# Two expert stages of a decoder kernel: inner rows made already turned, with the expanding weights fetched per row tile

## What is computed

```python
def moe_ff(x, gate_w, w1, w2, w3):            # layer L1_ffn: 8 experts, the best 2, inner width 512
    scores = xf @ gate_w
    topk_scores, topk_idx = jax.lax.top_k(scores, TOPK)
    topk_probs = jax.nn.softmax(topk_scores, axis=-1)
    ...
    h = jax.nn.silu(einsum('td,edh->eth', xf, w1)) * einsum('td,edh->eth', xf, w2)
    out_e = jnp.einsum('eth,ehd->etd', h, w3)
    out = jnp.einsum('etd,te->td', out_e, weight)
...
# layer L2_ffn: 8 experts, the best 1, inner width 1024
expert_idx = jnp.argmax(gate_probs, axis=-1)
for e in range(n_experts):
    ye = jax.nn.relu(x @ w1[e] + b1[e]) @ w2[e] + b2[e]
    out = out + jnp.where(sel, ye * expert_w[:, None], 0.0)
```

## Time and profile before

| | |
|---|---|
| median of three executions | 3069.21 us (3069.16 to 3077.27) |
| profiled execution, span from first to last instruction | 3070.0 us |
| TensorE busy | 2724.3 us, 89% of the span |
| VectorE, ScalarE, GpSimd busy | 1635.4, 1435.2, 1409.9 us |
| mean granted TensorE clock | 0.942 of full speed |
| moved by DMA | 106.09 MB, 35 GB/s on average |
| tile loop of stage a | 1369 to 1602 us, 39 tiles |
| tile loop of stage b | 2365 to 2553 us, 23 tiles |

### The profile page before, as it was taken

One profiled execution on the slowest core, in us unless ns is written; L12 is line 12 of the kernel. 1 busy time (PEld: TensorE's weight loads), 2 busy tenths in 40 slices (PEclk: granted clock), 3 DMA queues, 4 the chain that ended last, 5 costly groups with the idle time before them and its releaser, 6 DMA issues.

```text
span 3070.0 us, 70943 instructions
## 1 busy us (share of the span) xinstructions
PE 2724.3 (89%) x25041; PEld 2119.4 (69%) x25041; DVE 1635.4 (53%) x3572; ACT 1435.2 (47%) x4582; POOL 1409.9 (46%) x1645
## 2 busy tenths in 40 slices
PE   7888988569899979969986889999996996999999
PEld 6777776446666656746655767787774665768888
DVE  7999999654356645551126753333333224556643
ACT  4666665444366657733327852222321335773310
POOL 3777777723466755543335652332322223663320
PEclk9999998779999999969997989999995998999999
DMA  3000000100000000141111020000016111010100
GB/s 99 3 2 2 2 2 2 55 30 1 23 15 17 14 20 1 55 146 43 45 64 47 0 94 11 7 10 10 7 54 220 33 32 52 1 48 29 53 10 20
DMA packets 75141, 106.09 MB, mean 35 GB/s; under 512 B 11024, under 2 KB 54672, under 8 KB 74656
## 3 DMA queue, kind: packets, MB, share of 16 engines
q1 hardware_dynamic: 68960, 86.68, 8.5%
q0 software_dynamic: 5952, 16.26, 1.7%
HBM read 88.50 MB, written 14.42 MB: 34 GB/s over the span
## 4 chain that ended last, share of the span: by engine, by line
PE 55%; POOL 4%; DVE 4%; ACT 3%; issue 3%; SPq 1%; DMA 1%; DVEq 0%; ACTq 0%; POOLq 0%
PE up_ps L2490 5%; PE e_out_ps L2508 5%; PE t_ps L664 4%; PE s_ps L650 3%; PE bank_a L1554 3%; PE bank_b L1554 3%; POOL probs L569 2%; PE up_ps L2484 2%; PE bank_a L612 2%; ACT probs L798 2%; PE bank_d L701 2%; PE frame_ps L1633 2%; PE bank_d L620 2%; PE bank_b L1570 2%; PE bank_a L1570 2%
## 5 line engine op out<-in xcount | busy, mean ns | idle before, releaser
L569 POOL TENSOR_TENSOR probs<-probs,inv 128x512 f32<-128x512 f32 x320 | 328.0, 1039 | 274.1 <-DVE inv L919 273.9
L3454 POOL TENSOR_TENSOR hc<-h,bc 128x1024 f32<-128x1024 f32 x128 | 302.0, 2360 | 112.5 <-DVE h L3735 86.4
L798 ACT ACTIVATE probs<-s_ps,negmax 128x128 f32<-128x128 f32 (+1 forms) x768 | 297.7, 415 | 6.4 <-DVE negmax L879 5.0
L3735 DVE TENSOR_TENSOR_SCAN h<-da,dbu_ps 128x1024 f32<-128x1024 f32 x128 | 292.5, 2286 | 11.1 <-DVE dbu_ps L3747 4.4
L664 PE MATMUL t_ps<-ident,probs 128*128 128x128 f32 x1280 | 208.2, 286 | 57.8 <-POOL probs L569 49.2
L664 PEld LDWEIGHTS t_ps<-ident,probs 128*128 128x128 f32 x1280 | 139.2, 141 | 124.7 <-POOL probs L569 59.4
L3682 ACT ACTIVATE da<-dta_ps 128x1016 f32<-128x1016 f32 x128 | 130.3, 1018 | 150.2 <-PE dta_ps L3544 149.9
L3544 PE MATMUL dta_ps<-dt,a_spread 32*128 32x128 f32 x2048 | 155.2, 291 | 43.1 <-ACT da L3682 23.0
L2414 POOL DMA_INDIRECT expert_rows_out<-y,row_to x62 | 61.1, 986 | 268.7 <-DVE y L2773 138.3
L879 DVE TENSOR_REDUCE negmax<-s_ps 128x4 f32<-128x1024 f32 (+1 forms) x128 | 156.6, 1223 | 44.7 <-PE s_ps L650 42.7
L3544 PEld LDWEIGHTS dta_ps<-dt,a_spread 32*128 32x128 f32 x2048 | 130.4, 194 | 67.2 <-ACT da L3682 30.0
(11 more groups left out here) (509 smaller groups left out, 6752.4 us busy)
## 6 DMA issues: line engine op xcount, KB each, us to landing
cT<-in_ctx_turned SPq DMA_DIRECT2D x32, 256.0 KB, 2.6
w_down<-in_L_ffn_w SPq DMA_DIRECT2D x8, 1024.0 KB, 12.3
w_up<-in_L_ffn_w SPq DMA_DIRECT2D x8, 1024.0 KB, 13.5
c_in<-in_ctx SPq DMA_DIRECT2D x16, 256.0 KB, 2.8
w_gate<-in_L_ffn_w SPq DMA_DIRECT2D x8, 512.0 KB, 6.8
w_up<-in_L_ffn_w SPq DMA_DIRECT2D x8, 512.0 KB, 9.0
w_down<-in_L_ffn_w SPq DMA_DIRECT2D x8, 512.0 KB, 9.0
w_gate<-expert_rows_out SPq DMA_DIRECT2D x8, 512.0 KB, 6.6
```

What stands on the lines that cost most here:

```text
L569: pool.tensor_tensor(probs[:, u % 2, i], probs[:, u % 2, i], inv[:, u % 2, HB * i:HB * (i + 1)].unsqueeze(2).broadcast_to([P, HB, W]), ALU ...
L798: last = act.activation(probs[:, u % 2, i, k, :], src, ACT.Exp, bias=negmax[:, u % 2, at], accum_out=sums[:, u % 2, at])
L3454: pool.tensor_tensor(hc[:, s % 4], h[:, s % 2], bc[:, j, 1, :].unsqueeze(1).broadcast_to([P, 2 * G, P]), ALU.mult).then_inc(hc_ready.sem, 1)
L3735: dve.tensor_tensor_scan(flat(h[:, s % 2]), flat(da[:, s % 4]), dbu_ps[s % 2][:, :, :, :].rearrange("p i g t -> p (i g t)"), 0.0, ALU.mult ...
```

## The change

In `raise_up` the roles of the operands are exchanged. The weight is stationary, in blocks of 128x128 (`raise_part`), and the turned rows `xT` are moving, 128 columns. The result comes out with inner channels as partitions, as `bring_down` wants it, so that `turn_hidden`, the tile `hid` and the copies through it are gone: VectorE multiplies `up_ps` with `silu` into `hT` (stage a), ScalarE applies bias and ReLU from `up_ps` into `hT` (stage b). `bring_down(i-1)` follows `raise_up(i)` directly, and the loop has one step less.

The expanding weights (`w_gate`, `w_up`) are no longer loaded for all experts. SP reads the owner of tile i into a register and fetches that expert's weights from DRAM into one of three buffers `lift_sb` (two DMAs of 512 KB for a tile of stage a, one of 1024 KB for stage b), as soon as the tile three back has been raised. TensorE waits for them per tile. `w_down` is still loaded whole, and TensorE waits for it in step 1. `owner` is computed ahead of the copy from `held_ps`. `gathered` has SBUF of its own.

```diff
+LIFTS = 3
...
-        up_sb = far("w_up", [P, E, DC, HID])
-        gate_sb = sb("w_gate", [P, E, DC, HID]) if gated else None
...
+        raised = [w_gate, w_up] if gated else [w_up]
+        lift_sb = far("w_lift", [P, LIFTS, len(raised), DC, HID])
+        gathered = sb("gathered", [P, top, B, D])
...
-        for e in range(E):
-            beside += [(gate_sb[:, e], chunked(w_gate[e]))] if gated else []
-            weights += [(up_sb[:, e], chunked(w_up[e])), (down_sb[:, e], chunked(w_down[e]))]
...
+        weights = [(down_sb[:, e], chunked(w_down[e])) for e in range(E)]
+        early = weights[0:EARLY if after.weights_read else 0]
+        weights = weights[len(early):]
...
+            sp.wait_ge(owners.sem, owners.done(0))
+            for i in range(N):
+                e = sp.value_load(owner[0:1, i:i + 1], min_val=0, max_val=E - 1)
+                sp.wait_ge(upped.sem, upped.done(HALVES * (i - LIFTS) + HALVES - 1))
+                for k, w in enumerate(raised):
+                    sp.dma_start(lift_sb[:, i % LIFTS, k], w.rearrange("e (c p) n -> p e c n", p=P)[:, e]
+                                 ).then_inc(lifts[i % LIFTS].sem, 16)
...
-            def raise_up(i, e):
+            def raise_part(bank, k, i, half):
+                for m in range(4):
+                    at = half * 512 + m * P
+                    for cc in range(DC):
+                        last = pe.matmul(up_ps[:, bank, m, :], lift_sb[:, i % LIFTS, k, cc, at:at + P], xT[:, i % 2, cc, :],
+                                         start=(cc == 0), stop=(cc == DC - 1))
+                return last
+
+            def raise_up(i):
+                pe.wait_ge(lifts[i % LIFTS].sem, lifts[i % LIFTS].base + 16 * len(raised) * (i // LIFTS + 1))
                 pe.wait_ge(xT_ready.sem, xT_ready.done(B + i))
                 if gated:
                     pe.wait_ge(silued.sem, silued.done(i - 1))
...
+                    raise_part(1, 0, i, 0).then_inc(gate_made.sem, 1)
                 for half in range(HALVES):
                     pe.wait_ge(hT_ready.sem, hT_ready.done(HALVES * (i - 1) + half))
...
+                    raise_part(half, len(raised) - 1, i, half).then_inc(upped.sem, 1)
...
-            pe.wait_ge(loads.sem, all_loaded)
             pe.wait_ge(owners.sem, owners.done(0))
-            expert = {}
             turn_rows(0)
-            for i in range(N + 2):
+            for i in range(N + 1):
                 if i + 1 < N:
                     turn_rows(i + 1)
                 if i < N:
-                    expert[i] = pe.value_load(owner[0:1, i:i + 1], min_val=0, max_val=E - 1)
-                    raise_up(i, expert[i])
-                if 1 <= i <= N:
-                    turn_hidden(i - 1)
-                if i >= 2:
-                    bring_down(i - 2, expert.pop(i - 2))
+                    raise_up(i)
+                if i == 1:
+                    pe.wait_ge(loads.sem, all_loaded)
+                if i >= 1:
+                    bring_down(i - 1, pe.value_load(owner[0:1, i - 1:i], min_val=0, max_val=E - 1))
...
+            def take_up(i, e):
                 act.wait_ge(downed.sem, downed.done(i - 2))
                 for half in range(HALVES):
...
+                    act.wait_ge(upped.sem, upped.done(HALVES * i + half))
+                    for m in range(4):
+                        at = 4 * half + m
+                        last = act.activation(hT[:, i % 2, at, :], up_ps[:, half, m, :], ACT.Relu,
+                                              bias=b_up_sb[:, e, at:at + 1])
                     last.then_inc(hT_ready.sem, 1)
...
+            def multiply_up(i):
+                dve.wait_ge(downed.sem, downed.done(i - 2))
+                dve.wait_ge(silued.sem, silued.done(i))
+                dve.wait_ge(upped.sem, upped.done(i))
+                dve.tensor_tensor(hT[:, i % 2], up_ps[:, 0], silu[:, i % 2], ALU.mult).then_inc(hT_ready.sem, 1)
```

More of the change, by code:

```diff
@@ L2290, in sparse_expert_stage @@
         mixed = h_all if pre else gathered[:, 0]
[L2291 removed]
+        up_ps, turn_ps = ps("up_ps", [P, 2, 4, P]), ps("turn_ps", [P, 2, 4, P])
         out_ps = [ps("e_out_ps0", [P, 512]), ps("e_out_ps1", [P, 512])]
@@ L2318, in sparse_expert_stage @@
             gating += [(ns[:, :], norm_scale[:, :]), (nh[:, :], norm_shift[:, :])]
[L2319 removed]
         if b_up is not None:
[L2321 removed]
+            gating += [(b_up_sb[:, :, :], b_up.rearrange("e p m -> p e m")),
                        (b_down_sb[:, :, :], b_down.rearrange("e o d -> o e d").broadcast_to([P, E, D]))]
[L2323 to L2327 removed]
+        weights = [(down_sb[:, e], chunked(w_down[e])) for e in range(E)]
+        early = weights[0:EARLY if after.weights_read else 0]
+        weights = weights[len(early):]
         gate_loads = c("gate_loaded")
         gate_loaded = gate_loads.base + 16 * len(gating)
[L2330 removed]
+        all_loaded = loads.base + 16 * len(early + weights)
+        lifts = [c("w_landed0"), c("c_spread"), c("null_arg")]
         all_kept = kept.base + 16 * GROUPS
@@ L2336, in sync @@
                 sp.dma_start(dst, s).then_inc(gate_loads.sem, 16)
-            for dst, s in beside:
-                sp.dma_start(dst, s).then_inc(loads.sem, 16)
             for sem, value in after.weights_read:
@@ L2593, in scalar @@
             act.wait_ge(owners.sem, owners.done(0))
-            act.wait_ge(loads.sem, all_loaded)
             copy_rows(0)
-            for i in range(N + 1):
+            for i in range(N):
                 if i + 1 < N:
                     copy_rows(i + 1)
-                if gated and i < N:
+                if gated:
                     take_gate(i)
-                if i >= 1:
-                    e = act.value_load(owner[0:1, i - 1:i], min_val=0, max_val=E - 1) if b_up is not None else 0
-                    take_hidden(i - 1, e)
+                else:
+                    take_up(i, act.value_load(owner[0:1, i:i + 1], min_val=0, max_val=E - 1))
             def scale_first(b):
@@ L2753, in vector @@
                                      op0=ALU.add, op1=ALU.add).then_inc(rows_known.sem, 1)
-            def take_up(i):
-                dve.wait_ge(hid_turned.sem, hid_turned.done(HALVES * (i - 2) + HALVES - 1))
-                if gated:
-                    dve.wait_ge(silued.sem, silued.done(i))
-                for half in range(HALVES):
-                    dve.wait_ge(upped.sem, upped.done(HALVES * i + half))
-                    out = hid[:, i % 2, half * 512:(half + 1) * 512]
-                    if gated:
-                        last = dve.tensor_tensor(out, up_ps[:, 0, :], silu[:, i % 2, :], ALU.mult)
-                    else:
-                        last = dve.tensor_copy(out, up_ps[:, half, :])
-                    last.then_inc(hid_ready.sem, 1)
+            def multiply_up(i):
[3 more added lines that the diff above has]
+                dve.tensor_tensor(hT[:, i % 2], up_ps[:, 0], silu[:, i % 2], ALU.mult).then_inc(hT_ready.sem, 1)
             def take_out(i, e):
@@ L2778, in vector @@
             dve.wait_ge(owners.sem, owners.done(0))
-            dve.wait_ge(loads.sem, all_loaded)
-            for i in range(N + 2):
-                if i < N:
-                    take_up(i)
-                if i >= 2:
-                    e = dve.value_load(owner[0:1, i - 2:i - 1], min_val=0, max_val=E - 1) if b_down is not None else 0
-                    take_out(i - 2, e)
+            dve.wait_ge(gate_loads.sem, gate_loaded)
+            for i in range(N + 1):
+                if gated and i < N:
+                    multiply_up(i)
+                if i >= 1:
+                    e = dve.value_load(owner[0:1, i - 1:i], min_val=0, max_val=E - 1) if b_down is not None else 0
+                    take_out(i - 1, e)
             def mix(b):
@@ L2820, in sparse_expert_stage @@
         done = Later(y_ready, N - B)
-        loads.advance(16 * len(beside + early + weights))
+        loads.advance(16 * len(early + weights))
         gate_loads.advance(16 * len(gating))
@@ L2844, in sparse_expert_stage @@
             stored[k].advance(16 * ((N + 1 - k) // 2))
-        for n in (upped, hid_ready, hid_turned, hT_ready):
+        for n in (upped, hT_ready):
             n.advance(HALVES * N)
+        for k in range(LIFTS):
+            lifts[k].advance(16 * len(raised) * ((N + LIFTS - 1 - k) // LIFTS))
         for n in (downed, y_ready) + ((gate_made, silued) if gated else ()):
```

66 lines of the change are left out of this document (16 added, 50 removed).

## The result

| | before | changed |
|---|---|---|
| median, timed together | 3073.19 us (3069.16 to 3077.27) | 3047.69 us (3044.05 to 3049.2) |
| ratio | | 0.9911, 95% interval 0.9899 to 0.9923 |
| span of the profiled execution | 3070.0 us | 3047.0 us |
| timed a second time | 3073.05 us (3070.06 to 3081.44) | 3043.66 us (3038.38 to 3050.8), ratio 0.9898 (0.9878 to 0.9918) |

The forecast was 3043 us, 26 less than before. Measured were 25.5 less in the first series and 29.4 in the second. Of the 4.7 us between 3043 and 3047.69, 4.0 are the kernel before itself, which now came out at 3073.19 and not at 3069.21.

What follows compares the result with a forecast made beforehand. TensorE was taken to bound both tile loops. Loop savings of 11.5 and 16.7 us, with starts of +2.5 and -0.5, summed to -26.2 from the 3069.2 us median: 3043 us, range 3034 to 3048.

Steps and rivals of the forecast that it cites:

- The main term: Both tile loops: exchanged operands at 0.1117 us per record, transposes gone; -11.5 us in stage a, -16.7 in b.
- The loop of stage a: Stage a's tile loop: -0.30 us per tile over 39 tiles, -11.5 us, period 5.52.
- The starts: Ahead of the two loops: stage a +2.5 us with row fetches behind full queues, stage b -0.5.
- The prediction's own terms for stage a: Start of stage a: loop 0.2 to 3.1 us later, TensorE's own register load of 0.4 no longer there.
- Waits in the loop: Per-tile weight fetches: 5 to 10 us from release to landing, under 13.0 of slack in stage a; zero cost.
- Rival 1: At each start, row fetches wait behind all three weight-fetch pairs and land after 9.7 us: 3052 us, chance 0.09.
- Rival 2: In the loops, weight fetches come late: 3189 us, chance 0.06, or near no change, 0.04.
- Rival 3: Raising products: weight loads not hidden, a record costs 0.192 us instead of 0.1117: 3202 us, chance 0.02.
- Rival 4: Raising products: TensorE's sequencer cannot feed 16 products for 8 instructions, so nothing is saved: 3069 us, chance 0.02.

Runs made afterwards that it cites:

- both: Changed kernel with owners made ahead of in_row and weight fetches for tiles 1 and 2 held until two row fetches landed: 3042.15 us, ratio 0.9893.
- Rows first: Changed kernel with weight fetches for tiles 1 and 2 issued only after the first two row fetches landed: 3042.58 us, ratio 0.9895.

## Why the prediction was right

**The main term was right, and for the reason given.** The row of the last stage, 0.1117 us per fp32 record of 128 columns, carried over to the raising products to the hundredth: 3.57 us for 32. The transposes' 0.43 and 0.87 us went. The periods 5.52 and 7.24 are those forecast (5.52, 7.25).

**The loop of stage a gained 1.7 us more than forecast.** 0.30 x 39 are 11.7. The other 1.5 lie in the first tile, part of which runs at half clock (1.2 GHz) after TensorE's wait for the tables and rows. Before, the gate product began at 1372.08, and the next rows of that timeline are

```profile
1375.64 2.79 PE L2490 MATMUL up_ps<-w_up,xT 128*128 x4
1378.27 0.38 PE L2476 MATMUL x_ps<-ident,rows 128*128 128x128 f32 x2
```

The two products took 6.19 us (1372.08 to 1378.27), 2.8 more than at full clock; after the change the same tile takes 4.79, 1.2 more. The windows of these two stretches, before and then changed, give a granted clock of 0.56 and 0.73:

```profile
1372.08:1378.27 6.19, 6.19 (x8) 2.57 (x9) 0.00 (x0) 2.29 (x4) 0.78 (x1) 0.56 0.12 31
```
```profile
1382.75:1387.54 4.79, 4.79 (x33) 4.79 (x33) 0.00 (x0) 2.69 (x4) 0.94 (x1) 0.73 0.48 160
```

The kernel that only fetches, with the old products, takes 4.68 and has a loop of 231.1 us, also 1.5 shorter than before; the one that only exchanges starts as early as before, takes 6.38, and its loop is 11.6 shorter, as forecast. So it comes from when the full clock returns in relation to the first product, and not from the products. It returned 5.4 us after the first product before, 2.5 in the changed kernel, 2.5 with the fetch alone, 5.7 with the exchange alone. Counted from `in_tile` on VectorE it came after 22.3 to 22.9 us in eleven of the twelve traces (18.9 in "both"), though the loops began 17.0 to 20.3 us after it. By these numbers a start that is later by some microseconds costs only about half of them here. I had costed the first tile like any other.

**The starts.** Forecast +2.5 and -0.5, measured +2.8 and -0.24. The prediction's own terms for stage a, 3.1 less 0.4, give 2.7 and not 2.5. I chose the landing beside full queues, 5.8, against 2.9 beside empty ones; it was 6.5. "Rows first" and "both" show that the choice was one of queue volume, and that the lower end would have been right with one pair in flight that had left well ahead.

**Waits in the loop.** I put the time from release to landing at 5 to 10 us against a slack of 13.0. It was 5.8 (one buffer), with landings of 3.7/4.6/6.8 us in the changed kernel. Two buffers leave 2 x 5.52 - 3.57 = 7.5 us, and do not wait; one leaves 1.95, and waits 3.7. The relation of period and time to landing holds at all three.

**The rivals.** Rival 1, rows behind all three lifts, would have shown landings of 9.7 us: they were 6.5, while the last of the six lifts landed 8.6 us after its issue at most. Rival 2, late fetches, did not come about in the changed kernel. With one buffer it does, and there its price turned out to be set too low: I priced a late fetch by (L + 3.57)/3 alone, at full clock. The runs showed that TensorE loses clock by waiting, 2.2 us a tile on top of the 3.8 that the wait itself lengthened it by. Had the fetches been late in the changed kernel it would probably have been slower than the 3189 us of that rival; no run shows that case. Rival 3, weight loads not hidden: they last 194 ns and the records follow each other after 112, so they overlap. The Trainium skill's ratio of 2.5 (TensorE: Matmul & The Clock Gate, section "Back-to-back issue gap") is 3.57 to 3.44, or 1.04, for these fp32 products; the measurement decides. Rival 4 fell with the period.

**What does not add up to the microsecond.** The profile shows 23.0 us, the touched stretches 27.9, the medians 25.5 and 29.4. The differences are of the size by which untouched stages differ between executions, 5 us; nothing finer about this change can be read from times. The first median, 3047.69, lies 0.3 us inside the upper end of the range, the second, 3043.66, in its middle: that the forecast came so close to the second is luck, while the periods are not.

**Still open.** It was not tried what sets the moment at which the full clock comes back at a loop's start, nor why it came some 3.5 us sooner after `in_tile` in "both".

## What to carry to other kernels

If a product's result has to be turned before its next use, swap its operands so that it comes out turned; for fp32 the stream of narrow products cost here 4% more per column than wide ones, and the transposes and an eviction went. Price such a swap from a row of the same kernel with the same shape and type, wherever it stands. Weights that the swap forces to be fetched per tile were free here as long as the time from release to landing fitted the periods that the buffers leave and the volume stayed under what the queues move (391 GB/s): count it for 1, 2 and 3 buffers, and let the first small fetches of a stage leave ahead of the bulk.

## What the runs showed of the hardware that I had not expected

- **Idle time costs twice.** With 3.7 us of waiting per tile the granted clock averaged 0.79 and the 32 records that followed took 5.30 us, not 3.57. Filling the wait with useless products took 75 us off the kernel. Waits of 1.3 to 2.1 us in a tile of 9.2 left it at 0.97 to 1.00.
- **DMA reached 391 GB/s** in 50 us while TensorE was busy for 48.21 of them; I had taken 325 GB/s, the average of a burst of eight loads, for more of a limit than it is.
- **Small indirect fetches are delayed by the volume in the queues, not stopped by it**: 2.9 us beside one pair that is nearly through, 6.5 beside three just issued, though those three took longer themselves (4.3 to 8.6 us).
- **The untouched stages differ by 5 us** either way between executions; the largest part found is one stage that was granted 0.83 or 0.93 over the same 100 us and took 5.7 us longer.
- **Weights that have only just landed cost 0.10 us**, at the first weight load of the tile; full queues beside the products cost them nothing (3.57 us at 357 GB/s).
